# The second layer of a gated feed-forward stage with its weights stationary and its output turned back

## The chip, the cores and the metric

The kernel runs on one core of one Trainium2 chip. The metric is the time of one execution on the device, in microseconds (us). Busy times and orders of events come from a trace of one profiled execution.

## The reference

A small network works on x of shape 16 x 16 x 16 x 64: 4096 tokens of 64 channels, 16 images of 256 tokens. It has eight steps in a row, each preceded by a normalization and added to its input. The change touches the second, `L0_ffn`. It runs on 8 "rows" in its own set-up, but on 16 images here (s = 256 tokens, D = 64, H = 256):

```python
weights = (jnp.einsum('bsd,do->bso', x, wr) + br)[..., 0]
k = max(1, int(CAPACITY * s))
kk = k - 1 if k > 1 else 1
_, idx = jax.lax.top_k(weights, k)
sel_idx = idx[:, :kk]
sel = jnp.take_along_axis(x, sel_idx[:, :, None], axis=1)
h = jax.nn.gelu(jnp.einsum('bkd,dh->bkh', sel, w1) + b1)
y = jnp.einsum('bkh,hd->bkd', h, w2) + b2
w_sel = jnp.take_along_axis(weights, sel_idx, axis=1)
y = y * w_sel[..., None]
...
return processed + x
```

For each image the 127 tokens with the largest router weight go through a layer of 256 with a gelu and a layer back to 64, with the bias b2, and are scaled with the router weight. All is float32.

## The kernel before

All 4096 tokens stay in SBUF for the whole kernel, in X. They are worked on in 8 blocks of 512 tokens (BLK; four tiles t of 128 tokens, two images). The eight steps are eight stages s = 0 to 7, one after the other, each with its own body for every engine; a stage runs over the blocks two at a time: `trips` makes a hardware loop of three trips and a fourth trip written out, with u = 0 for even blocks and u = 1 for odd ones. Engines are ordered only by semaphores, and each executes its own instructions in the order written.

Besides the stage's own work each block carries two other things:

- The preparation of a block ahead (of b + 2, or of the next stage's first). VectorE takes the statistics of X (`prep_stats`), GpSimd makes rstd by a power (`prep`, L643), VectorE writes V (`prep_norm`, L1651), TensorE transposes V (`turn_v`, L1065), ScalarE copies it to VS (L701), and VectorE writes the rounding rest into VS's other half (`prep_split`, L1672), which raises vt_ready.
- A step of a power iteration on small matrices that a later stage needs, cut into pieces. TensorE has slot1 and slot2 in even blocks and slot3 in odd ones, each behind it a small copy by ScalarE (T, U, msum) and a segment on GpSimd: seg1 (ends with bsq, L500, which slot2 needs), seg2 (which slot3 needs) and seg3. GpSimd's order in an even block is seg1, rstd, seg2; in an odd block seg3, rstd.

The stage that is changed is `topk_stage` (s = 1). TensorE computes for a block the router row (rep_hi and rep_lo, into bank 2 + u), then the first layer with W1 stationary and 512 tokens moving (two halves c of the 256 hidden units, into banks 0 and 1), waits for vt_ready of the next block, issues slot1 or slot3, and then the second layer: `hid` holds gelu's output as [128 hidden, 512 tokens] for each c (L776, ScalarE), and for each tile t its 128 x 128 piece is the stationary operand and W2b the moving one, with b2 added by a matmul of one row of ones (L1139, L1140). So the output y comes with tokens on partitions, in bank 4 + u. VectorE meanwhile finds for each token by comparisons whether it is among the kept (L1735 to L1752), makes coef from it, XV = X + V, writes V of the block ahead, waits for l2_done, and computes X = XV + y * coef (L1757, L1759), which raises block_done. l2_done also tells ScalarE when `hid` may be overwritten.

`fold` is a [128, 64] matrix of two identities, one above the other (L1581): stationary data of [128, 128 tokens] with fold moving gives, for 128 tokens, the sum of the upper and the lower 64 rows, turned. Stages 3, 5 and 7 end with it (L1397). `ct` is a tile of the seventh stage.

Of the kernel before, what the change touches and what calls it, by code (L numbers as in the profile page):

```python
# [21 lines left out]
ACT = mybir.ActivationFunctionType  # L22
AX = mybir.AxisListType

P = 128
C = 64
IMG = 16
NT = 4
# [3 lines left out]
NB = 8  # L32
# [16 lines left out]
CREDIT = 2  # L49
# [22 lines left out]
def metaformer(nc, a, out):  # L72
    ctx = ExitStack()
    with ctx:
        def sb(name, shape, dt=F32):
            return ctx.enter_context(nc.sbuf_tensor(name, shape, dt))

        def sem(name):
            return ctx.enter_context(nc.semaphore(name))

        banks = ctx.enter_context(nc.psum_tensor("banks", [P, 8, 512], F32))
        bank = [banks[:, i, :] for i in range(8)]
# [32 lines left out]
        ones = sb("ones", [P, PIX])  # L115
# [32 lines left out]

        W2b = sb("W2b", [P, 2, C])
        b1b = sb("b1b", [P, 2])  # L150
        b2b = sb("b2b", [1, C])
        wrow = sb("wrow", [P, BLK])
        wcol = sb("wcol", [P, NT])
        above = sb("above", [P, NT])
# [3 lines left out]
        tmp = sb("tmp", [P, NT, C])  # L158
# [34 lines left out]
        hid = view(scratch, 0, (4, BLK))  # L193
# [17 lines left out]
        fold = sb("fold", [P, C])  # L211
# [16 lines left out]
        ct = sb("ct", [P, BLK])  # L228
# [51 lines left out]
        block_done = sem("block_done")  # L280
# [7 lines left out]
        h_ready = sem("h_ready")  # L288
        l2_done = sem("l2_done")
        y_ready = sem("y_ready")  # L290
        logits_ready = sem("logits_ready")
        lg_ready = sem("lg_ready")
        ex_ready = sem("ex_ready")
# [41 lines left out]
        def row(ap):  # L335
            return ap.rearrange("(o n) -> o n", o=1)

        def col(ap):
            return ap.rearrange("(n o) -> n o", o=1)

        def bcast(ap, n):
# [9 lines left out]
        ]  # L351
        loads = [
            (W2b[:], a["L0_ffn_w2"].rearrange("(n p) c -> p n c", p=P)),
            (b1b[:], a["L0_ffn_b1"].rearrange("(n p) -> p n", p=P)), (b2b[:], row(a["L0_ffn_b2"])),
            (omb[0:3 * TAPS, :], col(a["L1_conv_om_bias"])),
            (bg[3][:], bcast(a["L1_ffn_gate_b"], P)),
            (W2[3][:], a["L1_ffn_W2"].rearrange("e h c -> h e c")),
# [79 lines left out]
        def _(pool):  # L437
# [7 lines left out]

            pool.memset(OMK_cols[:].bitcast(F32), 0.0)
            pool.memset(omb[:], 0.0)
            pool.memset(W2[5][:], 0.0).then_inc(w2_zeroed, 1)
            pool.memset(ones[:], 1.0)
            pool.memset(neghalf[:], -0.5)  # L450
# [246 lines left out]
        def _(act):  # L697
# [79 lines left out]

            def topk_stage(i, s, s_next, wrap):
                for u in range(2):
                    for c in range(2):  # L780
                        hidden(i, u, s, c, ACT.Gelu_apprx_tanh, b1b[:, c:c + 1])
                    (slot1 if u == 0 else slot3)(i + STEP0[s])
                    if u == 0:
                        slot2(i + STEP0[s])
                    prep_ahead(i, u, s, s_next, wrap)
# [207 lines left out]
        def _(pe):  # L993
            pe.sem_inc(v_turned, CREDIT)
            pe.sem_inc(l2_done, 4)
            pe.sem_inc(s_used, 3)


# [2 lines left out]
            for k in range(TAPS):  # L1001
                ins = pe.transpose(bank[k // 8][0:C, (k % 8) * C:(k % 8 + 1) * C], Ko[:, :, k], ident[0:C, 0:C])
# [121 lines left out]
            def topk_stage(i, s, s_next, wrap):  # L1124
                for u in range(2):
                    b = i * 2 + u
                    pe.wait_ge(vt_ready, b + (NB * s + 1))
                    pe.wait_ge(block_done, b + (NB * s + 1))
                    exact(bank[2 + u][:, :], rep_hi[:, 2, :], rep_lo[:, 2, :], u).then_inc(b_row, 1)
                    for c in range(2):  # L1130
                        pe.wait_ge(h_ready, i * 4 + (2 * u + c + 1))
                        exact(bank[c][:, :], W1_hi[1][:, c, :], W1_lo[1][:, c, :], u).then_inc(h_psum, 1)
                    pe.wait_ge(vt_ready, b + (NB * s + 2))
                    (slot1 if u == 0 else slot3)(i + STEP0[s])
                    pe.wait_ge(h_ready, i * 4 + (2 * u + 2 + CREDIT))
                    for t in range(NT):
                        y = bank[4 + u][:, t * C:(t + 1) * C]
                        for c in range(2):
                            pe.matmul(y, hid[:, 2 * u + c, t * P:(t + 1) * P], W2b[:, c, :], start=(c == 0), stop=False)  # L1139
                        ins = pe.matmul(y, ones[0:1, 0:P], b2b[:], start=False, stop=True)  # L1140
                    ins.then_inc(l2_done, 2)
                    if u == 0:
                        slot2(i + STEP0[s])
                    pe.wait_ge(ch_act, i * 3 + (3 * STEP0[s] + 4 + u))
                    prep_ahead(prep, i, u, s, s_next, wrap)
# [399 lines left out]
        def _(vec):  # L1545
            steps = [0]

            def mark(ins):

                steps[0] += 1  # L1550
                ins.then_inc(vec_step, 1)
# [5 lines left out]
            def link(ins):  # L1557

                mark(ins)
                settle()  # L1560
# [170 lines left out]
            def topk_stage(i, s, s_next, wrap):  # L1731
                for u in range(2):
                    b = i * 2 + u
# [12 lines left out]
                    for t in range(NT):  # L1746
# [5 lines left out]
                    mark(vec.scalar_tensor_tensor(coef[:], above[:], float(KEEP), wcol[:], ALU.is_lt, ALU.mult))  # L1752
                    link(vec.tensor_tensor(XV[:], xblock(b), V[u][:], ALU.add))
                    ahead(prep_norm, i, u, s, s_next, wrap)
                    vec.wait_ge(l2_done, i * 4 + (2 * u + 2 + 4))
                    settle()
                    link(vec.tensor_tensor(tmp[:], bank[4 + u][:, 0:NT * C].rearrange("p (t c) -> p t c", t=NT),  # L1757
                                           coef[:].rearrange("p (t o) -> p t o", o=1).to_broadcast([P, NT, C]), ALU.mult))
                    vec.tensor_tensor(xblock(b), XV[:], tmp[:], ALU.add).then_inc(block_done, 1)  # L1759
                    ahead(prep_split, i, u, s, s_next, wrap)  # L1760
# [290 lines left out]
```

## Time and profile before

| | |
|---|---|
| median of 3 runs | 1260.85 us (1257.79 to 1271.09) |
| the profiled execution | 1254.95 us, span 1253.2 us |
| mean granted TensorE clock | 0.841 |
| TensorE busy | 993.4 us (79%) |
| VectorE busy | 705.2 us (56%) |
| ScalarE busy | 478.2 us (38%) |
| GpSimd busy | 458.7 us (37%) |
| group L1139, TensorE, 128 records | 32.7 us in the stage |
| group L1140, TensorE, 64 records | 20.5 us in the stage |

A float32 matmul leaves two records on TensorE. Weight loads (PEld) overlap the matmuls. "Idle before <- X" says how long the engine had been idle and what released it. Line numbers are those of this kernel.

### The profile page before, as it was taken

The numbers are of one execution on the slowest core, as the hardware profiler recorded it, in microseconds if no ns is written. First come the engines' busy times: TensorE is split into PE (matmuls) and PEld (weight loads), VectorE is DVE, ScalarE is ACT, GpSimd is POOL, SyncE is SP. The second block draws the span as 40 slices with busy tenths as digits, with TensorE's granted clock in tenths as the row PEclk, the third lists the DMA queues.
The fourth block names the chain that finished last, engine by engine and source line by source line (L and its number), as shares of the span: only waits on it lengthen the run. The fifth ranks groups of instructions, "written<-read, shape, count | busy, mean of one in ns | idle before, by whom it ended". The sixth has DMA issues, their size and how long they took to land.

```text
span 1253.2 us, 17519 instructions
## 1 busy us (share of the span) xinstructions
PE 993.4 (79%) x4690; PEld 607.0 (48%) x4690; DVE 705.2 (56%) x2469; ACT 478.2 (38%) x903; POOL 458.7 (37%) x1308
## 2 busy tenths in 40 slices
PE   2444368877789899888888987779899566899998
PEld 2444356665455455554444444545555444444443
DVE  3555756554455555544366565667665543666653
ACT  1222201113544555544254444433434111466665
POOL 4555535654054333454542431125554310111010
PEclk9999999555799987988976787787877766899999
DMA  4400000000000000000000000000000000000000
GB/s 72 78 0 0 1 1 0 0 1 1 1 1 1 0 0 0 0 0 2 1 1 0 0 0 1 0 1 1 0 0 1 0 0 1 1 9 4 8 4 9
DMA packets 26340, 6.27 MB, mean 5 GB/s; under 512 B 24054, under 2 KB 26230, under 8 KB 26294
## 3 DMA queue, kind: packets, MB, share of 16 engines
q1 hardware_dynamic: 26294, 5.73, 2.5%
q8 instruction: 20, 0.33, 0.1%
q14 instruction: 26, 0.21, 0.1%
HBM read 4.68 MB, written 1.05 MB: 5 GB/s over the span
## 4 chain that ended last, share of the span: by engine, by line
PE 44%; issue 13%; DVE 10%; ACT 4%; POOL 2%; DVEq 0%; ACTq 0%; POOLq 0%
PE banks L1373 7%; PE banks L1200 6%; PE banks L1091 4%; PE banks L1092 3%; PE banks L1022 3%; PE banks L1500 3%; PE banks L1390 2%; PE banks L1397 2%; PE banks L1192 2%; DVE V L1651 2%; PE banks L1341 2%; DVE weighted L1913 2%; DVE summed L1917 2%; PE banks L1155 1%; PE banks L1176 1%
## 5 line engine op out<-in xcount | busy, mean ns | idle before, releaser
L903 ACT ACTIVATE scratch<-banks,b 128x512 f32<-128x512 f32 x224 | 144.6, 683 | 57.1 <-PE banks L1092 53.9
L1373 PE MATMUL banks<-scratch,W 128*64 128x512 f32 (+1 forms) x448 | 157.3, 688 | 0.5
L1808 DVE TENSOR_TENSOR scratch<-banks,XR 128x1024 f32<-128x1024 f32 x72 | 87.5, 1224 | 103.5 <-PE banks L1192 76.5
L1091 PE MATMUL banks<-VS,W_hi 128*128 128x512 f32 x240 | 121.8, 507 | 2.2 <-DVE X L1982 1.0
L643 POOL TENSOR_TENSOR rstd<-vareps,neghalf 128x4 f32<-128x4 f32 x64 | 67.5, 1054 | 136.8 <-DVE vareps L1639 131.2
L701 ACT ACTIVATE VS<-banks 64x256 fp32r<-64x256 f32 x112 | 42.5, 379 | 190.2 <-PE banks L1065 175.0
L1065 PE MATMUL banks<-ident,V 128*128 128x128 f32 x128 | 33.1, 348 | 93.8 <-DVE V L1651 90.7
L1092 PE MATMUL banks<-VS,W_lo 128*128 128x512 f32 x240 | 107.3, 447 | 0.0
L1913 DVE SCALAR_TENSOR_TENSOR weighted<-banks,b,cwide 128x512 f32<-128x512 f32 x72 | 53.9, 749 | 86.4 <-PE banks L1373 85.8
L1651 DVE TENSOR_SCALAR V<-X,moments,rstd 128x64 f32 (+1 forms) x256 | 62.9, 309 | 57.1 <-POOL rstd L643 35.5
L1200 PE MATMUL banks<-scratch,region 128*64 128x256 f32 x576 | 90.3, 440 | 3.6 <-DVE scratch L1808 3.6
L914 ACT ACTIVATE cwide<-banks 128x512 f32<-128x512 f32 x96 | 57.4, 598 | 86.7 <-PE banks L1390 86.4
L1091 PEld LDWEIGHTS banks<-VS,W_hi 128*128 128x128 f32 x240 | 51.6, 215 | 53.8 <-issue 28.6
L1672 DVE TENSOR_TENSOR VS<-banks,VS 64x256 fp32r<-64x256 f32 x112 | 47.4, 423 | 52.4 <-ACT VS L701 50.8
L1065 PEld LDWEIGHTS banks<-ident,V 128*128 128x128 f32 x128 | 15.4, 164 | 119.5 <-DVE V L1651 82.4
L652 POOL TENSOR_TENSOR ex<-euler,lg 128x32 f32<-128x32 f32 x8 | 43.5, 5432 | 80.2 <-DVEq L1875 80.0
L558 POOL TENSOR_TENSOR cp<-U,qv 64x18 f32<-64x18 f32 x40 | 8.8, 239 | 147.4 <-ACT U L739 147.4
L655 POOL TENSOR_TENSOR ex<-euler,m 128x4 f32<-128x4 f32 x16 | 16.3, 1020 | 119.8 <-DVEq L1883 119.8
L1200 PEld LDWEIGHTS banks<-scratch,region 128*64 128x64 f32 x576 | 38.8, 151 | 40.6 <-issue 25.1
L1092 PEld LDWEIGHTS banks<-VS,W_lo 128*128 128x128 f32 x240 | 53.0, 221 | 6.4
L1390 PE MATMUL banks<-cwT,select 16*128 16x512 f32 x96 | 54.0, 563 | 1.1 <-ACT cwT L908 1.1
L1373 PEld LDWEIGHTS banks<-scratch,W 128*64 128x64 f32 (+1 forms) x448 | 33.6, 156 | 40.1 <-issue 25.9
(280 smaller groups left out, 2114.9 us busy)
## 6 DMA issues: line engine op xcount, KB each, us to landing
X<-in_x SPq DMA_DIRECT2D x8, 128.0 KB, 2.6
region<-in_L_ffn_W SPq DMA_DIRECT2D x2, 512.0 KB
out<-X SPq DMA_DIRECT2D x8, 128.0 KB, 2.0
W<-in_L_ffn_W SPq DMA_DIRECT2D x1, 512.0 KB
region<-in_L_ffn_W SPq DMA_DIRECT2D x2, 256.0 KB
scratch<-in_L_conv_kernel SPq DMA_DIRECT2D x2, 144.0 KB
W<-in_L_ffn_W SPq DMA_DIRECT2D x1, 256.0 KB
region<-in_L_ffn_w SPq DMA_DIRECT2D x2, 128.0 KB
```

The lines of the kernel that those rows point to most:

```text
L643: pool.tensor_tensor(rstd[:], vareps[:], neghalf[:], ALU.pow).then_inc(rstd_ready, 1)
L903: act.activation(hid[:, c % 4, :], bank[c % 2][:, :], ACT.Gelu, bias=b1[s][:, w:w + 1]).then_inc(h_ready, 1)
L914: act.activation(cwide[:, j, :], bank[4][:, :], ACT.Copy).then_inc(wide_copied, 1)
L1065: ins = pe.transpose(bank[6][:, m * P:(m + 1) * P], V[u][:, 2 * m:2 * m + 2, :].rearrange("p t c -> p (t c)"), ident[:])
L1091: pe.matmul(out, hi, VS[u][:], start=True, stop=False)
L1092: return pe.matmul(out, lo, VS[u][:], start=False, stop=True)
L1200: ins = pe.matmul(bank[1][m * C:(m + 1) * C, 0:PIX], Z[v][:, 2 * m + h, k * C:(k + 1) * C], S[:, k % 3, h, m * PIX:(m + 1) * PIX], start=( ...
L1373: ins = pe.matmul(y, W2[s][:, w, :], hid[:, c % 4, :], start=opens, stop=closes, skip_group_check=True)
L1390: pe.matmul(bank[4][:, :], select[:, j, :], cwT[:], start=True, stop=True).then_inc(wide_psum, 1)
L1651: ins = vec.tensor_scalar(V[u][:, place, :], X[:, bass.ds(b * NT + t, 1), :].rearrange("p o c -> p (o c)"), moments[:, t, 0:1], rstd[:, t: ...
L1808: vec.tensor_tensor(S[:, k % 3], pair(p), xr, ALU.mult).then_inc(s_ready, 1)
L1913: vec.scalar_tensor_tensor(weighted[:] if j else summed[u][:], bank[2 + j % 2][:, :], b2[s][:, j:j + 1], cwide[:, j, :], ALU.add, ALU.mult ...
```

## The change

W2b becomes the stationary operand: for each half c of the hidden units one matmul with 64 columns takes `hid` of 512 tokens as the moving operand, and writes into 64 of the 128 partitions of bank 5 (c = 0 the lower, c = 1 the upper). ScalarE copies the bank to `ct` and adds b2 on the way; b2b is now a column of 128 with zeros in its second half, so that it is added once. Four matmuls with `fold` sum the two halves and turn them back, into bank 4 for every block. Two new semaphores, pair_copied and pair_turned, carry the hand-over.

```diff
-        b2b = sb("b2b", [1, C])
+        b2b = sb("b2b", [P, 1])
...
+        pair_copied = sem("pair_copied")
+        pair_turned = sem("pair_turned")
...
-            (b1b[:], a["L0_ffn_b1"].rearrange("(n p) -> p n", p=P)), (b2b[:], row(a["L0_ffn_b2"])),
+            (b1b[:], a["L0_ffn_b1"].rearrange("(n p) -> p n", p=P)), (b2b[0:C], col(a["L0_ffn_b2"])),
...
+            pool.memset(b2b[:], 0.0)
...
             def topk_stage(i, s, s_next, wrap):
                 for u in range(2):
+                    b = i * 2 + u
                     for c in range(2):
                         hidden(i, u, s, c, ACT.Gelu_apprx_tanh, b1b[:, c:c + 1])
                     (slot1 if u == 0 else slot3)(i + STEP0[s])
+                    act.wait_ge(l2_done, i * 4 + (2 * u + 2 + 4))
+                    act.wait_ge(pair_turned, b + 1)
+                    act.activation(ct[:], bank[5][:, :], ACT.Identity, bias=b2b[:]).then_inc(pair_copied, 1)
                     if u == 0:
                         slot2(i + STEP0[s])
...
+            pe.sem_inc(pair_turned, 1)
...
                     pe.wait_ge(h_ready, i * 4 + (2 * u + 2 + CREDIT))
+                    for c in range(2):
+                        pe.matmul(bank[5][c * C:(c + 1) * C, :], W2b[:, c, :], hid[:, 2 * u + c, :],
+                                  start=True, stop=True, skip_group_check=True).then_inc(l2_done, 1)
+                    pe.wait_ge(pair_copied, b + 1)
+                    pe.wait_ge(block_done, b + (NB * s + CREDIT))
                     for t in range(NT):
-                        y = bank[4 + u][:, t * C:(t + 1) * C]
-                        for c in range(2):
-                            pe.matmul(y, hid[:, 2 * u + c, t * P:(t + 1) * P], W2b[:, c, :], start=(c == 0), stop=False)
-                        ins = pe.matmul(y, ones[0:1, 0:P], b2b[:], start=False, stop=True)
-                    ins.then_inc(l2_done, 2)
+                        ins = pe.matmul(bank[4][:, t * C:(t + 1) * C], ct[:, t * P:(t + 1) * P], fold[:],
+                                        start=True, stop=True)
+                    ins.then_inc(pair_turned, 1)
...
-                    vec.wait_ge(l2_done, i * 4 + (2 * u + 2 + 4))
+                    vec.wait_ge(pair_turned, b + 2)
                     settle()
-                    link(vec.tensor_tensor(tmp[:], bank[4 + u][:, 0:NT * C].rearrange("p (t c) -> p t c", t=NT),
+                    link(vec.tensor_tensor(tmp[:], bank[4][:, 0:NT * C].rearrange("p (t c) -> p t c", t=NT),
```

On TensorE, in an even block of the stage's loop, slot1's matmuls, the second layer and slot2 stand like this before (a row is one instruction, or several alike; `scratch` is hid, and REGISTER_ALU computes the value of a wait):

```order
L1022 MATMUL banks<-va,Ko 64x2 x9
L1135 REGISTER_ALU
L1139 MATMUL banks<-W2b,scratch 128x64 [waits h_ready]
L1139 MATMUL banks<-W2b,scratch 128x64
L1140 MATMUL banks<-b2b,ones 128x64
L1139 MATMUL banks<-W2b,scratch 128x64 x2
L1140 MATMUL banks<-b2b,ones 128x64
```

And in the changed kernel, whose lines are numbered 7 to 10 higher here:

```order
L1030 MATMUL banks<-va,Ko 64x2 x9
L1143 REGISTER_ALU
L1145 MATMUL banks<-scratch,W2b 64x512 [waits h_ready]
L1145 MATMUL banks<-scratch,W2b 64x512
L1147 REGISTER_ALU
L1150 MATMUL banks<-fold,ct 128x64 [waits block_done,pair_copied]
L1150 MATMUL banks<-fold,ct 128x64 x3
```

Of 12 matmuls 6 are left, between the same neighbours, with one wait among them.

On ScalarE, in the same even block, from the second gelu to the copy of V's transposes, before:

```order
L776 ACTIVATE scratch<-banks,b1b 128x512 [waits l2_done,h_psum]
L730 ISA
L731 ACTIVATE T<-banks 64x18 [waits ch_pe]
L736 REGISTER_ALU
L738 ACTIVATE U<-banks 64x9 [waits ch_pe]
L739 ACTIVATE U<-banks 64x18
L712 ISA
L701 ACTIVATE VS<-banks 64x2x128 [waits v_turned]
```

And in the changed kernel:

```order
L779 ACTIVATE scratch<-banks,b1b 128x512 [waits l2_done,h_psum]
L733 ISA
L734 ACTIVATE T<-banks 64x18 [waits ch_pe]
L787 REGISTER_ALU
L788 ISA [waits l2_done]
L789 ACTIVATE ct<-banks,b2b 128x512 [waits pair_turned]
L739 REGISTER_ALU
L741 ACTIVATE U<-banks 64x9 [waits ch_pe]
L742 ACTIVATE U<-banks 64x18
```

One copy of a whole bank is put between T (slot1's result) and U (slot2's), with no table load beside it.

## Rows read from the trace of the kernel before

**Rows 1.** Busy time in five blocks: stretch, length, each engine's busy us (instructions), PEclk, DMA
```profile
175.69:191.24 15.55, 15.15 (x72) 13.00 (x72) 9.48 (x45) 2.56 (x7) 3.94 (x11) 1.00 0.00 1
...
207.30:222.30 15.00, 14.59 (x73) 12.30 (x73) 10.19 (x47) 2.56 (x7) 6.42 (x23) 0.72 0.00 0
222.30:238.77 16.47, 11.28 (x39) 9.19 (x39) 8.68 (x44) 2.33 (x5) 12.33 (x38) 0.50 0.00 0
238.77:254.57 15.80, 15.39 (x72) 13.03 (x73) 10.19 (x47) 2.56 (x7) 6.53 (x24) 0.50 0.00 0
...
286.08:296.73 10.65, 9.15 (x38) 7.26 (x39) 7.55 (x33) 4.03 (x7) 7.66 (x25) 0.66 0.00 1
```

**Rows 2.** Timeline, TensorE, block 4 (start us, us, engine, line, tiles, count)
```profile
244.93 1.12 PE L1139 MATMUL banks<-W2b,scratch 128*128 128x64 f32 x4
...
251.57 0.58 PE L1042 MATMUL banks<-bsq,ones 64*128 64x2 f32 x2
```

**Rows 3.** Timeline, the other engines in block 4
```profile
248.34 0.19 POOL L500 TENSOR_TENSOR bsq<-vb 64x2 f32<-64x2 f32 x1
...
249.83 0.98 DVE L1651 TENSOR_SCALAR V<-X,moments,rstd 128x64 f32 x4 [1.62 <-POOL rstd L643]
251.68 0.42 DVE L1757 TENSOR_TENSOR tmp<-banks,coef 128x256 f32<-128x256 f32 x1 [0.87 <-PE banks L1140]
...
254.28 0.17 ACT L739 ACTIVATE U<-banks 64x18 f32<-64x18 f32 x1
```

**Rows 4.** Waits in block 3 (who waited for whom: us, times, longest)
```profile
DVE V L1651 <- POOL rstd L643: 6.0, 1, 6.0
...
PE banks L1065 <- DVE V L1651: 5.2, 1, 5.2
```

**Rows 5.** Timeline, block 2
```profile
216.86 0.19 POOL L500 TENSOR_TENSOR bsq<-vb 64x2 f32<-64x2 f32 x1
...
219.30 0.58 PE L1042 MATMUL banks<-bsq,ones 64*128 64x2 f32 x2
```

**Rows 6.** Timeline, TensorE, a later stage, granted clock 0.50
```profile
664.99 1.80 PE L1397 MATMUL banks<-fold,summed 128*128 128x64 f32 x8
666.73 0.79 PE L1390 MATMUL banks<-cwT,select 16*128 16x512 f32 x1
...
670.96 1.98 PE L1373 MATMUL banks<-scratch,W 128*64 128x512 f32 x4
672.87 0.79 PE L1390 MATMUL banks<-cwT,select 16*128 16x512 f32 x1
```

**Rows 7.** Timeline, TensorE: two groups at the full clock, one full-width matmul at half
```profile
642.54 1.08 PE L1373 MATMUL banks<-scratch,W 128*64 128x512 f32 x4
...
648.09 1.10 PE L1397 MATMUL banks<-fold,summed 128*128 128x64 f32 x8
...
908.93 2.05 PE L1373 MATMUL banks<-scratch,W 128*128 128x512 f32 x2
```

**Rows 8.** Timeline, the third stage: hand-overs from TensorE to ScalarE and back
```profile
300.84 0.68 ACT L790 ACTIVATE omt<-banks,omb 64x512 f32<-64x512 f32 x1 [9.03 <-PE banks L1155]
...
301.69 1.91 PE L1161 MATMUL banks<-fold_quads,omt 64*128 64x32 f32 x8
...
320.59 3.74 PE L1155 MATMUL banks<-VP,OMK_cols 128*64 128x512 f32 x9
...
324.37 0.68 ACT L790 ACTIVATE omt<-banks,omb 64x512 f32<-64x512 f32 x1 [2.63 <-PE banks L1155]
```

**Rows 9.** Timeline, the end of block 7 and the next stage's start
```profile
295.75 0.42 DVE L1757 TENSOR_TENSOR tmp<-banks,coef 128x256 f32<-128x256 f32 x1 [1.29 <-PE banks L1140]
...
304.02 1.33 POOL L643 TENSOR_TENSOR rstd<-vareps,neghalf 128x4 f32<-128x4 f32 x1 [0.17 <-POOL qv L494]
...
306.23 0.88 DVE L1651 TENSOR_SCALAR V<-X,moments,rstd 128x64 f32<-128x64 f32 x4
```

**Rows 10.** Timeline, ScalarE, block 7
```profile
290.53 1.28 ACT L978 ACT_TABLE_LOAD   x1
```

## What was predicted, before the changed kernel had run

> **What bounds the kernel now.** The change touches one of eight stages, the token gate's feed-forward part (`topk_stage`, "the stage" below), which runs from 175.7 to 296.6 us: eight blocks, an even one (u=0) and an odd one (u=1) in turn. I read first the busy time by block [rows 1]. A block takes 15.0 to 16.5 us whatever its kind. In even blocks TensorE is busy almost throughout (15.39 of 15.80 us), in odd ones it is not (11.28 of 16.47), while GpSimd is busy 12.33 us of the odd block and 6.53 of the even one. So two different chains set the two kinds of block, and the change can be worth something only where TensorE's does.
>
> Then the order of time in block 4, an even one [rows 2, 3]. TensorE's second layer, the group that the change replaces, runs from 244.93 until the next instruction starts at 251.57: 6.64 us for 12 matmuls, which leave 24 records. Right behind it come slot2 (251.57 on), ScalarE's copy of U (ends 254.45) and the transposes of the block after next (254.57, the end of this window in [rows 1]). Nothing in between waits for another engine: GpSimd had bsq, which slot2 needs, at 248.53, and VectorE had V, which the transposes need, at 250.81. VectorE waited 0.87 us for the group. The even block is TensorE's chain, and the group is on it.
>
> In block 3, an odd one, the waits [rows 4] tell another story: V waited 6.0 us for GpSimd's rstd, and the transposes waited 5.2 us for V. GpSimd was in seg3, which starts when slot3's result is copied; slot3 is issued ahead of the second layer. The group could be 5 us shorter or longer there and nothing would move.
>
> The clock: the granted clock of [rows 1] is 0.50 (1.2 GHz) in blocks 3 and 4 and partly higher in 2 and 7. Block 0 is listed at 1.00, but is as long as block 4 (15.55 against 15.80), so I take the slow durations for it too. In block 2 the fast stretch was worth some 0.5 to 0.8 us (15.00 against 15.55 and 15.80).
>
> **The change, part by part.** Prices are those of the slow clock, from rows of later stages that do the same thing.
>
> 1. Removed: 12 matmuls on the array, 6.64 us per block [rows 2].
> 2. Added: two matmuls with W2 stationary, 64 columns each, 512 activations moving, into the two column halves. An expert pair (L1373) is exactly this. In the slow clock its four records take 1.98 us [rows 6]. One matmul of the full 128 columns took 2.05 us for two records [rows 7], so the halves cost together what one full matmul costs; I take 1.98.
> 3. Added: the wait for ScalarE and back. The nearest case is omt (L790), Identity with a bias from PSUM. TensorE's last matmul ended at 324.33 and ScalarE started at 324.37; it took 0.68 us for 512 columns; in the slow clock TensorE's next load started 0.17 us after such a copy ended [rows 8]. Together 0.04 + 0.68 + 0.17 = 0.89 us.
> 4. Added: four fold products. L1397 has that shape: 1.80 us, 1.74 until the next instruction starts [rows 6]. Its first load was ahead of time there, and with the wait it won't be; the four turns behind omt took 1.91 [rows 8]. I take 1.85.
> 5. Sum: 1.98 + 0.89 + 1.85 = 4.72 us against 6.64, so 1.92 us less per block.
>
> ScalarE is cheap to use: it is busy 2.56 us of an even block [rows 1]. Behind the new copy on its queue stand U's copy in even blocks, whose matmuls are later on TensorE anyway, and the next VS copy in odd ones, which waits for the transposes. Behind the copy of block 7 stands a table load, needed only in the next stage [rows 10]. No other table load is added.
>
> The single bank 4 makes the fold products wait for block_done of the block before. That came before vt_ready of the next block, on which TensorE already waits ahead of slot1 or slot3, because VectorE splits after it adds. So this costs nothing; if VectorE came late it would be seen first at vt_ready. VectorE's own wait moves from l2_done to pair_turned, same place. The memset of one more column and a load of 64 small pieces in place of one row are hidden: they belong to the loads at the kernel's start, and the stage starts at 175.7 us.
>
> *Even blocks.* After the cut slot2 would start at 251.57 - 1.92 = 249.65 in block 4. bsq is there at 248.53. The transposes would come at 252.65, V is there at 250.81. VectorE's tmp would start right behind V, at about 250.9, still ahead of the next block. So the whole 1.92 us comes through, and what is late next is slot2 behind bsq, 1.1 us further down. Block 2 is the tightest: its group began in a fast stretch, slot2 at 219.30 and bsq done at 217.05 [rows 5], with room for about 2.1 us. Four even blocks: 4 x 1.92 = 7.7 us.
>
> *Odd blocks.* Blocks 1, 3 and 5: 0.
>
> *Block 7* has no block to prepare in this stage; its output starts the next one. VectorE waited 1.29 us for the group there [rows 9], so 1.29 is the most that can be won before VectorE's own work is the end. A part of it meets GpSimd: in the next stage rstd ended at 305.35 and V started 0.88 us later, so no more than 0.9 passes. Its group ran partly fast, where the cut is smaller. I take 0.5.
>
> **Sum:** 7.7 + 0.5 = 8.2 us off the profiled execution's 1254.95 us, so 1246.7. The median of the runs is 5.9 us above that execution; off the median it is 1252.6 us, 0.65% less.
>
> *Bounds of the unknown prices.* High price: give the way to ScalarE and back 1.7 us and the group is 5.5, worth 1.1 per even block, 4.4 in all. Low price: at the full clock the pair takes 1.08 and the fold products 1.10 [rows 7]; a group of 3.0 would save 3.6, but slot2 then stands behind bsq (room of 3.0 us in block 4, 2.2 in block 2), so at most 2.2 to 3.0 per even block, about 11, and 12 with block 7.
>
> A rule that would price item 2 otherwise: TensorEngine Tiling in the Trainium skill says under Key Properties that changing the tiling mode drains TensorE, and this change makes it switch to half-width tiles and back in every block. The rows of the expert pair contain both switches already (a full-width matmul before and after), so the sum stays at 1.98; if the drain were extra, it would eat into the 1.92.
>
> **The rivals.**
>
> *A, the forecast:* even blocks gain, odd ones don't. 8 us, between 4 and 11. Chance 0.68.
>
> *B, the clock comes up as well.* The pair streams 512 columns where the old matmuls streamed 64, behind the first layer's six 512-column streams. The fast stretches of blocks 2 and 7 [rows 1] followed such streams. If each of the four even blocks got one, that is 4 x 0.7 = 2.8 more, 11; if it held through slot1, the group and slot2, the odd blocks' start up to slot3 would shorten too, 13 to 20 off: 1241 to 1248. For: the denser stream. Against: a new gap of 0.9 us, then 64-column products and slot2 again. TensorE: Matmul & The Clock Gate in the Trainium skill (Part 1) has it that activity releases the throttle, and that small idle times between groups can make it swing; so it speaks for both. Chance 0.14.
>
> *C, nothing to be seen:* a gain under 4 us, because the group is nearer 5.7, or the fast stretches of blocks 2 and 7 are lost (about 1.5 us), or the room before bsq is eaten. 1257 to 1261. Chance 0.13.
>
> *D, slower.* The hand-over through ScalarE costs more than the group saved: this decides from 0.89 + 1.92 = 2.8 us between the pair's end and the first fold product. If ScalarE had to change tables for Identity and back for Gelu (1.28 us each [rows 10]), in each even block 2.6 us would be added to TensorE's chain, 4 x (2.6 - 1.9) = 3 us slower, about 1264. Against: Copy runs between Gelus in this stage, and Identity beside Exp and Copy in the next, without loads, and the program has none. Chance 0.05.
>
> **The numbers.** I call 1% (12.6 us) what can be told from no change here. A and C stay within it; of B somewhat more than half passes it, and A's tail with a lucky median a little, so faster 0.13; D passes it only if the loads also stall the odd blocks, slower 0.03; the rest, 0.84, within. The range: up to 1260 it holds A, most of C; down to 1243 it holds most of B.
>
> **What would show it.** Right: in even blocks the group takes about 4.7 us, of which 0.9 between pair and fold products; even blocks of about 13.5 to 14 us, odd ones still 16; V's wait for rstd in odd blocks as before, TensorE's wait for V there near 7 us in place of 5. Block 7's tmp no longer waits. Stages after it as long as before. Wrong: slot2 waiting for GpSimd in even blocks (my room was too small); a granted clock above 0.6 over most of the stage (B); fold products starting over 1.5 us after the pair (C or D); odd blocks that change their length by more than 0.5 us at the same clock.

## The result and the profile after

The changed kernel takes 1250.43 us (median of 20 runs, 1243.67 to 1260.70), the kernel before 1264.59 us in 20 runs beside them. The ratio is 0.9929, with a 95% interval of 0.9899 to 0.9958: 0.7% faster, 9 us. It is less than the 14.2 us between the two medians, because all ratios here compare fast runs alone, those within 1.5% of the fastest of their kernel, and six of the 20 runs before are slower than that. The forecast was 8.2 us less (0.65%) and 1252.6 us.

The profiled execution of the changed kernel has a span of 1245.2 us against 1253.2. Here is the busy time by block, as in [rows 1]: blocks 0, 2, 3, 4 and 7, the columns being the stretch, its length, and the busy time (instructions) of TensorE, its weight loads, VectorE, ScalarE and GpSimd, then the granted clock and DMA.

```profile
175.72:188.54 12.82, 11.53 (x60) 9.08 (x61) 9.39 (x45) 3.24 (x8) 4.22 (x11) 0.75 0.00 1
...
204.52:218.47 13.95, 12.65 (x60) 9.42 (x61) 10.10 (x47) 3.25 (x8) 6.20 (x23) 0.50 0.00 0
218.47:235.02 16.55, 8.52 (x27) 5.57 (x27) 8.76 (x44) 3.02 (x6) 12.33 (x39) 0.50 0.00 0
235.02:248.95 13.93, 12.63 (x60) 9.40 (x61) 10.10 (x47) 3.24 (x8) 6.20 (x23) 0.50 0.00 0
...
278.98:289.38 10.40, 8.51 (x26) 5.59 (x27) 7.54 (x33) 4.83 (x8) 7.11 (x23) 0.50 0.00 1
```

Block 4, wholly at the slow clock in both kernels, went from 15.80 to 13.93 us. Block 3, an odd one, went from 16.47 to 16.55, though TensorE has 2.8 us less to do in it. The stage takes 113.7 us in place of 121.0.

Block 4 in TensorE's order of time, where [rows 2] stood before, and ScalarE's copy:

```profile
241.18 1.97 PE L1145 MATMUL banks<-scratch,W2b 128*64 128x512 f32 x4
244.05 1.97 PE L1150 MATMUL banks<-fold,ct 128*128 128x64 f32 x8 [0.89 <-ACT ct L789]
245.95 0.58 PE L1050 MATMUL banks<-bsq,ones 64*128 64x2 f32 x2
```

```profile
243.31 0.69 ACT L789 ACTIVATE ct<-banks,b2b 128x512 f32<-128x512 f32 x1 [1.84 <-PE banks L1145]
```

The group takes 4.77 us from its first matmul to slot2 (245.95 - 241.18): 1.97 for the pair, 0.89 idle for the hand-over (TensorE gives the bank to ScalarE and gets ct back), the rest the fold products.

The limits that come next in block 4, where [rows 3] stood, on GpSimd and VectorE:

```profile
244.59 0.19 POOL L503 TENSOR_TENSOR bsq<-vb 64x2 f32<-64x2 f32 x1
```

```profile
246.08 0.99 DVE L1662 TENSOR_SCALAR V<-X,moments,rstd 128x64 f32 x4 [1.62 <-POOL rstd L646]
246.97 0.42 DVE L1768 TENSOR_TENSOR tmp<-banks,coef 128x256 f32<-128x256 f32 x1
```

bsq is there at 244.78, 1.2 us before slot2 takes it; VectorE no longer waits for the output. And the waits of block 3, where [rows 4] stood:

```profile
PE banks L1073 <- DVE V L1662: 7.1, 1, 7.1
DVE V L1662 <- POOL rstd L646: 6.0, 1, 6.0
```

V still waits 6.0 us for rstd, and what TensorE saved it now spends on waiting for V (7.1 us, before 5.2).

### The profile page after: what moved, and what is told of

Its sections match the earlier page's. It is cut to its first block, busy times and chain, and to the rows that moved or that the text cites. A ratio compares the mean times of both kernels' runs of the same rounds, so it can differ in the third digit from the quotient of the medians.

```text
span 1245.2 us, 17359 instructions
## 1 busy us (share of the span) xinstructions
PE 968.5 (78%) x4594; PEld 581.0 (47%) x4594; DVE 704.5 (57%) x2469; ACT 484.4 (39%) x911; POOL 459.9 (37%) x1309
## 3 DMA queue, kind: packets, MB, share of 16 engines
HBM read 4.68 MB, written 1.05 MB: 5 GB/s over the span
## 4 chain that ended last, share of the span: by engine, by line
PE 45%; issue 12%; DVE 9%; ACT 4%; POOL 4%; DVEq 0%; ACTq 0%; POOLq 0%
PE banks L1384 7%; PE banks L1211 6%; PE banks L1099 4%; PE banks L1030 3%; PE banks L1100 3%; PE banks L1511 2%; PE banks L1401 2%; PE banks L1203 2%; DVE V L1662 2%; PE banks L1408 2%; PE banks L1352 2%; PE banks L1166 1%; PE banks L1199 1%; PE banks L1187 1%; PE banks L1195 1%
## 5 line engine op out<-in xcount | busy, mean ns | idle before, releaser
L1384 PE MATMUL banks<-scratch,W 128*64 128x512 f32 (+1 forms) x448 | 154.2, 666 | 0.4
L1073 PE MATMUL banks<-ident,V 128*128 128x128 f32 x128 | 33.4, 352 | 102.6 <-DVE V L1662 99.5
L1073 PEld LDWEIGHTS banks<-ident,V 128*128 128x128 f32 x128 | 15.7, 165 | 129.7 <-DVE V L1662 90.8
```

The lines of the kernel that those rows point to most:

```text
L1073: ins = pe.transpose(bank[6][:, m * P:(m + 1) * P], V[u][:, 2 * m:2 * m + 2, :].rearrange("p t c -> p (t c)"), ident[:])
L1384: ins = pe.matmul(y, W2[s][:, w, :], hid[:, c % 4, :], start=opens, stop=closes, skip_group_check=True)
```

## Experiments

Below, a stage's length runs from block 1's transposes (the last that the stage before issues) to the next stage's first matmul, and a block's from the transposes that its predecessor issues to those that it issues itself; block 7 ends with the next stage's first matmul. The table is worked out from the starts of L1073 (L1065 before) in each kernel's trace.

```
kernel                              stage   block 0     1     2     3     4     5     6     7
before                              121.0     15.56 16.05 15.00 16.47 15.80 15.99 15.52 10.65
changed                             113.7     12.82 15.98 13.95 16.55 13.93 16.47 13.56 10.40
e1 new group in even blocks         115.5     13.69 16.53 13.02 15.92 13.97 16.47 13.56 12.35
e2 new group in odd blocks          120.3     15.56 15.61 15.81 16.55 15.79 15.93 15.51  9.50
e3 bias on VectorE, old operands    109.5     12.83 16.29 12.84 15.97 12.86 15.98 12.77  9.95
e4 changed, rstd ahead of seg3      104.9     12.80 10.65 16.91 10.66 16.97 10.66 16.72  9.50
e5 changed, no hand-over            109.3     12.81 15.96 12.99 16.51 12.97 15.61 12.81  9.66
e6 changed, odd pair three times    113.5     12.81 16.50 13.95 16.50 13.94 16.02 13.55 10.19
e7 changed, even pair twice         117.2     14.34 15.60 15.71 16.51 13.77 15.61 15.26 10.40
e8 changed, rstd ahead, two stages  106.6     13.70 10.66 16.95 10.66 16.94 10.66 16.59 10.40
e9 before, one bias matmul          114.3     12.81 16.50 13.94 16.51 13.93 16.51 13.62 10.47
e10 before, bias with 128 rows      116.2     12.93 16.50 14.65 16.50 14.48 15.92 14.18 11.03
e11 before, rstd ahead, two stages  109.0     14.65 11.21 16.95 11.21 16.71 11.22 16.74 10.31
e12 e3, rstd ahead, two stages      105.4     12.81 10.65 16.99 10.66 16.96 10.66 16.72  9.95
```

Lengths of one kind of block differ by 0.5 to 1.1 us where a stretch ran at the full clock. Each row is one profiled execution. e5, e6, e7 and e10 ran only that once, so for them there are blocks and stages but no ratio.

### Even blocks or odd ones

e1 has the new group under `if u == 0:` and the old one under `else:`, e2 the reverse. The new group stands where the diff has "...". In both, b2 is loaded in both forms, and the semaphores count only the blocks that use them:

```diff
+                    if u == 0:
...
+                    else:
+                        for t in range(NT):
+                            y = bank[4 + u][:, t * C:(t + 1) * C]
+                            for c in range(2):
+                                pe.matmul(y, hid[:, 2 * u + c, t * P:(t + 1) * P], W2b[:, c, :], start=(c == 0), stop=False)
+                            ins = pe.matmul(y, ones[0:1, 0:P], b2row[:], start=False, stop=True)
+                        ins.then_inc(l2_done, 2)
```

> The new group only in even blocks, the old one in odd blocks (and so in block 7). Stage lengths are from block 1's transposes to the next stage's first matmul: 121.0 us in the kernel before, 113.7 in the changed one. If the gain comes from TensorE's chain in the even blocks alone, all of it is here: the stage takes about 114 us (even blocks 13.9, odd ones 16 to 16.5), and the whole 8 us less than before. If every shortened group counts alike, there is half of it: about 117.4 us and 4 us less.

> The reverse: the new group only in odd blocks. If odd blocks wait for GpSimd's seg3, nothing is gained: the stage takes 120.5 to 121.5 us (block 7 may give 0.3 of it), the time is that of the kernel before. If every shortened group counts alike: about 117.4 us and 4 us less.

e1: 0.9923 of the kernel before (0.9885 to 0.9961), the same as the whole change. e2: 1.0006 (0.9972 to 1.0039), nothing. The blocks say it more sharply: block 4 takes 13.97 us in e1 and 15.79 in e2; block 3 takes 15.92 in e1, with the old group, and 16.55 in e2, with the new one, where e1 had a fast stretch in it (granted clock 0.61 against 0.50). So the gain is TensorE's chain in even blocks. The stage of e2 is 120.3 us, 0.2 below what was expected; its block 7, with the new group, took 9.50 us against 10.65.

The stage of e1 was to be about 114 us and is 115.5. The 1.9 us over the changed kernel's stage are block 7: 12.35 us with the old group, 10.40 with the new one; the differences of the other blocks cancel. VectorE's wait for the old group in e1's block 7:

```profile
290.22 0.42 DVE L1781 TENSOR_TENSOR tmp<-banks,coef 128x256 f32<-128x256 f32 x1 [3.00 <-PE banks L1161]
```

It is 3.00 us where the profiled execution before had 1.29 [rows 9], because part of that group had run at the full clock. At the slow clock the change is worth 1.95 us in block 7, up to the next stage's first matmul. Little of that is left further on. The next stage's first transposes, which wait for V, came 21.60 us after block 7's start in e1 (300.45 - 278.85) and 21.06 in the changed kernel (300.04 - 278.98): 0.54 us, and e1 ran partly at the full clock in between.

```profile
300.45 0.41 PE L1075 MATMUL banks<-ident,V 128*128 128x128 f32 x2 [2.44 <-DVE V L1672]
```

```profile
300.04 0.66 PE L1073 MATMUL banks<-ident,V 128*128 128x128 f32 x2 [3.24 <-DVE V L1662]
```

In the changed kernel V waits there for GpSimd's rstd:

```profile
298.91 0.99 DVE L1662 TENSOR_SCALAR V<-X,moments,rstd 128x64 f32<-128x64 f32 x4 [0.56 <-POOL rstd L646]
```

### More work in the groups

e6 adds two more pairs of W2 matmuls ahead of the pair in odd blocks, whose result the pair overwrites; e7 adds one pair, in even blocks (2 * 1 if u == 0).

```diff
+                    for c in range(2 * 2 if u == 1 else 0):
+                        pe.matmul(bank[5][c % 2 * C:(c % 2 + 1) * C, :], W2b[:, c % 2, :], hid[:, 2 * u + c % 2, :],
+                                  start=True, stop=True, skip_group_check=True)
```

> The changed kernel, and in odd blocks the pair of matmuls is issued three times (3.8 us more on TensorE in each odd block; the same result). TensorE waited 7.1 us for V there, so blocks 1, 3 and 5 keep their 16 to 16.5 us and the wait falls to about 3.3. Block 7, also odd, prepares nothing and has no such room: it takes the 3.8 us, 14.2 in place of 10.4. The stage: about 117.5. If odd groups counted like even ones, it would be 113.7 + 4 x 3.8 = 129.

> The changed kernel, and in even blocks the pair of matmuls is issued twice (1.9 us more in each). If TensorE's chain sets the even blocks all of it shows: 15.8 us in place of 13.9, the stage 121.3, as long as in the kernel before. If there is room in the even blocks too, less.

e6: with two pairs more, blocks 1, 3 and 5 keep their 16.0 to 16.5 us. The two pairs took 3.5 us in block 3, but the last pair and the fold products ran at the full clock (1.11 and 1.10 us in place of 1.98 and 1.97), so TensorE had only 1.8 us more to do there, and its wait for V fell to 5.4 us, not to 3.3. Block 7 didn't behave as expected: it stayed at 10.19 us, and the stage at 113.5 in place of 117.5. Its three pairs ran at the full clock (eight records in 1.94 us, and TensorE's fold products in 1.11), so the extra work cost little there.

```profile
283.14 1.94 PE L1145 MATMUL banks<-scratch,W2b 128*64 128x512 f32 x8 [0.52 <-ACT scratch L779]
284.91 1.03 PE L1148 MATMUL banks<-scratch,W2b 128*64 128x512 f32 x4
286.75 1.11 PE L1153 MATMUL banks<-fold,ct 128*128 128x64 f32 x8 [0.81 <-ACT ct L789]
```

e7: 1.76 us more in block 2 (13.95 to 15.71), 1.70 in block 6 and 1.52 in block 0, nearly the 1.9 expected. But block 4 took 13.77 us, less than without the extra pair. After the second pair its fold products and slot2 ran at the full clock (slot2's 18 records in 1.27 us, against 2.08 in the slow clock):

```profile
245.66 1.88 PE L1148 MATMUL banks<-scratch,W2b 128*64 128x512 f32 x4
248.44 1.10 PE L1153 MATMUL banks<-fold,ct 128*128 128x64 f32 x8 [0.90 <-ACT ct L789]
249.48 0.38 PE L1050 MATMUL banks<-bsq,ones 64*128 64x2 f32 x2
249.79 1.27 PE L1030 MATMUL banks<-vb,Ki 64*64 64x2 f32 x18
```

This speaks for rival B's mechanism, that a longer wide stream can bring the clock up. In e6 all four odd blocks had a fast stretch from the third pair or earlier, where the changed kernel had one in block 1 alone. But that is not shown: each kernel was profiled once, fast stretches also came in block 5 of e2, e5 and e10, which have no extra pair, and the granted clock over the stage is 0.62 in e6 but 0.57 in e7, against 0.56 in the changed kernel. In e7 the extra pair paid for itself in one block of four, and the stage took 117.2 us against 113.7. In the changed kernel the granted clock was 0.50 in blocks 2 to 7, and the stage owes nothing to it but in blocks 0 and 1.

### What the group is made of

e5 takes the hand-over out: the fold products read a constant tile, ScalarE's copy runs beside them.

```diff
-                    pe.wait_ge(pair_copied, b + 1)
...
-                        ins = pe.matmul(bank[4][:, t * C:(t + 1) * C], ct[:, t * P:(t + 1) * P], fold[:],
+                        ins = pe.matmul(bank[4][:, t * C:(t + 1) * C], before[:].rearrange("p t n -> p (t n)")[:, t * P:(t + 1) * P], fold[:],
...
+                    pe.wait_ge(pair_copied, b + 1)
                     pe.wait_ge(ch_act, i * 3 + (3 * STEP0[s] + 4 + u))
```

> The changed kernel, but the fold products read a tile of constants in place of ct, so they need not wait for ScalarE (the copy still runs); this leaves the second layer's output out. The group shrinks by the hand-over of 0.89 us, from 4.77 to about 3.9. In even blocks slot2 then meets its next limit, GpSimd's bsq: with the bias on VectorE the even blocks were 12.84 us and slot2 waited for GpSimd. So the even blocks should go from 13.9 to 12.9 to 13.1 us, the odd ones stay at 16 to 16.5, the stage comes to 109.5 to 110.5. If the hand-over was hidden anyway, nothing moves (113.7).

Block 4 took 12.97 us against 13.93, 0.96 less for a hand-over of 0.89; the stage 109.3. In block 4 bsq was there only 0.2 us before slot2 (243.48 and 243.70). The hand-over is on the path in full. That is the price of letting ScalarE stand between the two products.

e3 keeps the old operands and only drops the four bias matmuls per block:

```diff
-                                pe.matmul(y, hid[:, 2 * u + c, t * P:(t + 1) * P], W2b[:, c, :], start=(c == 0), stop=False)
-                        ins = pe.matmul(y, ones[0:1, 0:P], b2b[:], start=False, stop=True)
+                                ins = pe.matmul(y, hid[:, 2 * u + c, t * P:(t + 1) * P], W2b[:, c, :], start=(c == 0), stop=(c == 1))
...
                     link(vec.tensor_tensor(tmp[:], bank[4 + u][:, 0:NT * C].rearrange("p (t c) -> p t c", t=NT),
+                                           b2b[:].rearrange("p (o c) -> p o c", o=1).to_broadcast([P, NT, C]), ALU.add))
+                    link(vec.tensor_tensor(tmp[:], tmp[:],
```

> The kernel before with the hidden activations still stationary; only the four bias matmuls per block are gone, VectorE adds b2 with one instruction more (0.43 us) before it multiplies. Eight of twelve matmuls are left, 16 of 24 records, 4.43 us at the slow clock against 4.77 measured for the new group. If only the length of TensorE's group in even blocks matters, this gains as much as the change or slightly more: even blocks 13.6 us, the stage 112.5 to 113.5 us, the whole 8 to 9 us less than before. If the turned operands themselves bring the gain (wide moving streams, a better clock), it is below 4 us.

e3: 0.9905 (0.9869 to 0.9941), and the stage is 109.5 us, 4 us shorter than in the changed kernel and below what was expected. Whole times don't tell the two apart (0.9929 for the change). The eight matmuls alone took 3.67 us, not the 4.43 of their share. In block 6, where they ran faster still, slot2 met the limit named in the prediction: it waited 1.23 us for GpSimd.

```profile
239.75 3.67 PE L1139 MATMUL banks<-W2b,scratch 128*128 128x64 f32 x16
243.44 0.59 PE L1042 MATMUL banks<-bsq,ones 64*128 64x2 f32 x2
```

```profile
272.29 0.56 PE L1042 MATMUL banks<-bsq,ones 64*128 64x2 f32 x2 [1.23 <-POOLq L553]
```

So of the old group's 6.64 us the four bias matmuls, with one row of ones each, were 2.97, or 0.74 apiece, more than the 0.46 of a W2 matmul with 128 rows. The change's gain in the group is all theirs: turning the operands replaced 3.67 us by 4.77, and only because the bias went to ScalarE does the new group come out 1.87 us shorter. Two more kernels ask why they are dear. e10 leaves them in place and gives them all 128 rows (ones[:, 0:P] and a tile that is zero below its first row). e9 uses one of 256 columns that opens the bank (b2b then holds b2 four times):

```diff
+                    pe.matmul(bank[4 + u][:, 0:NT * C], ones[0:1, 0:P], b2b[:], start=True, stop=False, skip_group_check=True)
                     for t in range(NT):
                         y = bank[4 + u][:, t * C:(t + 1) * C]
                         for c in range(2):
-                            pe.matmul(y, hid[:, 2 * u + c, t * P:(t + 1) * P], W2b[:, c, :], start=(c == 0), stop=False)
-                        ins = pe.matmul(y, ones[0:1, 0:P], b2b[:], start=False, stop=True)
+                            ins = pe.matmul(y, hid[:, 2 * u + c, t * P:(t + 1) * P], W2b[:, c, :], start=False,
+                                            stop=(c == 1), skip_group_check=True)
```

> The kernel before, where the four bias matmuls stay in their places but take all 128 rows: ones as the stationary operand, and a tile with b2 in its first row and zeros below as the moving one. The same count of matmuls, columns and records. If the one-row shape between full ones is what costs, each of the four now costs what a W2 matmul costs, 0.46 us: a group of 5.4 to 5.6 us in place of 6.64, even blocks about 14.7. If it is only their number, 6.64 and 15.8 stay.

> The kernel before, where one bias matmul of one row and 256 columns opens the whole bank and the eight W2 matmuls add to it, in place of four bias matmuls of 64 columns between them. The eight alone took 3.67 us at the slow clock, with the four between them 6.64, so each of the four cost 0.74 us, more than the 0.46 of a W2 matmul. If what costs is going to one row and back, which now happens once in a block: a group of 4.4 to 4.6 us, even blocks about 13.7 us, as good as the changed kernel without a copy on ScalarE. If the columns cost, the one matmul costs as much as the four together and nothing is won (6.6).

e10's group, from block 4, two of its four tiles and the next instruction:

```profile
242.27 1.11 PE L1140 MATMUL banks<-W2b,scratch 128*128 128x64 f32 x4
243.18 0.64 PE L1141 MATMUL banks<-b2b,ones 128*128 128x64 f32 x2
...
247.02 0.64 PE L1141 MATMUL banks<-b2b,ones 128*128 128x64 f32 x2
247.58 0.58 PE L1043 MATMUL banks<-bsq,ones 64*128 64x2 f32 x2
```

It takes 5.31 us (247.58 - 242.27), 1.33 less than with one row, for the same number of matmuls, columns and records (5.4 to 5.6 was expected; even blocks behind the first took 14.2 to 14.7 us). The weight loads show a difference. With one row, in the kernel before, the bias matmul's load and the next W2 load begin no earlier than their matmuls do (245.98 and 246.59); in e10 the bias matmul's load begins 0.10 us ahead of its matmul (243.08 and 243.18):

```profile
245.98 0.50 PEld L1140 LDWEIGHTS banks<-b2b,ones 1*128 1x128 f32 x2
246.59 0.93 PEld L1139 LDWEIGHTS banks<-W2b,scratch 128*128 128x128 f32 x4
```

```profile
243.08 0.55 PEld L1141 LDWEIGHTS banks<-b2b,ones 128*128 128x128 f32 x2
```

e9's group:

```profile
241.49 1.22 PE L1136 MATMUL banks<-b2b,ones 1*128 1x256 f32 x2
242.63 3.67 PE L1140 MATMUL banks<-W2b,scratch 128*128 128x64 f32 x16
246.24 0.58 PE L1042 MATMUL banks<-bsq,ones 64*128 64x2 f32 x2
```

4.75 us (246.24 - 241.49), a little over the 4.4 to 4.6 expected, and 0.9924 of the kernel before (0.9892 to 0.9957): as good as the change, with neither a turned output nor a copy on ScalarE. The one-row shape between full ones costs 0.33 us each time in the slow clock (1.33 / 4). TensorEngine Tiling in the Trainium skill (Key Properties) says that changing the tiling mode drains TensorE. If a one-row matmul is such a change, e10 and the loads agree with that, but no run here tells a drain from another reason why the load isn't taken ahead. Nor does one isolate it for the half-width tiles of the new pair, whose 1.97 us includes it.

### Odd blocks, and a faster kernel

e4 moves one call on GpSimd in this stage; e8 does so in the first stage too (`()` in place of `(0,)`). seg3 then comes behind the step that makes rstd.

```diff
             def body(i, s, s_next, wrap):
...
-                    if s in (0, 1) and second_half:
+                    if s in (0,) and second_half:
                         seg3(step)
...
-                    if s not in (0, 1) and second_half:
+                    if s not in (0,) and second_half:
                         seg3(step)
```

> The changed kernel, and in this stage GpSimd computes rstd for the block ahead before seg3 in place of behind it. If odd blocks are set by seg3 ahead of rstd, V and the transposes come some 5 us earlier there, until slot1 of the next block waits for seg3's end: 3 to 3.6 us less in each of blocks 1, 3 and 5, the stage about 103 to 105 us and the whole 9 to 11 us less than the changed kernel (some 18 less than before). If something else holds the odd blocks, or seg3's later start by 1.4 us costs as much as the earlier V gives, nothing: the stage stays at 113 to 115 us.

> The changed kernel with rstd ahead of seg3 on GpSimd in this stage and in the first one, whose odd blocks have the same order. In this stage as with the change in this stage alone (104.9 us, odd blocks 10.7, even ones 16.9). If the first stage's odd blocks also wait for rstd behind seg3, it gets some us shorter and the whole falls below 1240; if not, the time is that of the kernel with the move in one stage, 0.986 of before.

e4: 0.9864 of the kernel before (0.981 to 0.9918), the stage 104.9 us. The odd blocks fall from 16.5 to 10.66 us, the even ones rise to 16.9, since seg3's end is now waited for by slot1 and bsq comes later:

```profile
204.35 0.38 PE L1044 MATMUL banks<-ones 64*128 64x1 f32 x2 [1.75 <-POOLq L618]
...
213.03 0.58 PE L1050 MATMUL banks<-bsq,ones 64*128 64x2 f32 x2 [1.28 <-POOLq L556]
```

A pair of blocks takes 27.6 us against 30.5. That shows what held the odd blocks. The even blocks' 3 us were not in the expectation as such, but its sum was right (3 us less for each pair). e8: 0.9738 (0.9687 to 0.979), median 1229.09 us, the fastest kernel of this study. In the first stage the odd blocks' transposes had waited 11.19 us for V and now wait 5.61. In e8, the transposes of an even block and then those of the odd one behind it:

```profile
42.72 0.69 PE L1073 MATMUL banks<-ident,V 128*128 128x128 f32 x2 [0.41 <-ACT U L742]
55.73 0.69 PE L1073 MATMUL banks<-ident,V 128*128 128x128 f32 x2 [5.61 <-DVE V L1662]
```

In the changed kernel these two started at 42.75 and 61.34, so 5.6 us came off each of three such blocks. The changed stage took 106.6 us in e8, not the 104.9 of e4, because blocks 0 and 7 had no fast stretch of that size.

e11 and e12 ask what the second layer's group is worth once GpSimd's order is mended: e11 is the kernel before with the same move, e12 is e3 with it.

> The kernel before, with its old second layer, and rstd ahead of seg3 in both stages. With the new group and this move, slot2 waited 1.3 us for GpSimd's bsq in even blocks: bsq came 5.9 us after slot1's end, because GpSimd was late. The old group takes 6.64 us, only some 0.7 us longer than that. So the change is worth at most 0.7 us in each of the four even blocks here and about 2 in block 7, 3 to 5 us in all in place of 8 to 9: 0.977 of before, against 0.974 with the new group. If the change keeps its worth whatever GpSimd does, it is 0.981.

> Rstd ahead of seg3 in both stages, and the kernel before's second layer without its bias matmuls, b2 added on VectorE. Its group takes 3.67 us against 4.77 of the new one, but in even blocks both end before bsq, so they should be alike: even blocks 16.9 us, odd ones 10.7, the time within 1 us of the kernel with the new group (0.974 of before). If the group still mattered there, 4 us less.

In the stage, e11 takes 109.0 us, e8 106.6, e12 105.4. The old group costs 0.55 us in each of three odd blocks (11.2 against 10.66) and little or nothing in blocks 2, 4 and 6, where slot2 waits for GpSimd with the new one. So within the stage the change is worth 2.4 us here, in place of 7.4. That is less, as expected, but below the 3 to 5 us of the expectation and made up otherwise: it had 0 for odd blocks (measured 1.7 in all) and about 2 for block 7 (measured -0.1, where e11 had a fast stretch). e12's blocks 1 to 6 are those of e8 to 0.1 us or so, as expected.

The whole times say something else: e11 is at 0.9809 (0.9784 to 0.9833), which is the 0.981 that the expectation gave to the rival, that the change keeps its worth. e12 is at 0.9757 (0.9733 to 0.9781), e8 at 0.9738, and e8's interval and e11's just overlap. e11 and e12 ran beside each other, e8 at another time on another chip. Between e11's and e8's profiled executions 12 us differ, of which only 2.4 lie before the third stage; the other 10 are in stages with the same instructions. Those stages, first in e8, then in e11:

```profile
265.61:1223.40 957.79, 815.04 (x3886) 458.57 (x3886) 532.98 (x1705) 426.10 (x742) 304.99 (x799) 0.83 0.01 2
```

```profile
268.00:1235.50 967.50, 828.91 (x3886) 462.74 (x3886) 533.51 (x1705) 425.32 (x742) 304.46 (x798) 0.82 0.01 2
```

The same 3886 records kept TensorE busy 14 us longer in e11, at a lower granted clock (0.82 against 0.83), while VectorE, ScalarE and GpSimd took what they took in e8. So the 10 us go with TensorE's clock, and are not work that the old group adds. In e12 those stages took 964.2 us. Two of e8's runs had the granted clock of e11's (0.82) and took 1234.1 and 1234.2 us, 3 to 4 us less than e11's median of 1237.7, which is nearer to the stage's 2.4. Why the clock was granted less in all of e11's runs (1236 to 1243 us) stays open, and so does what the change is worth in the whole time with this order on GpSimd.

## Why the prediction was right

**What bounds the stage.** Right on both kinds of block. Even blocks are TensorE's chain (e1, e5, e7's block 2), odd ones GpSimd's seg3 ahead of rstd (e2, e6, e4).

**The group.** Expected 4.72 us, measured 4.77: pair 1.98 and 1.97, hand-over 0.89 and 0.89, fold products 1.85 and 1.90. The pair came from a row of the same shape and clock. The 1.85 was a choice between 1.74 (same shape, first load ahead of time) and 1.91 (another shape). The hand-over's sum was right by luck, its parts were not. Expected were 0.04 us from the pair's end to ScalarE, 0.68 for the copy and 0.17 back; measured in block 4 are 0.16 (243.15 to 243.31), 0.69 and 0.05 (244.00 to 244.05). The 0.17 was not the way back alone: when that load started [rows 8], TensorE was still in L1176's matmuls (301.32 to 301.76).

**What passes through.** Expected 1.92 in each even block, 7.7 in four. Measured 2.74, 1.05, 1.87 and 1.96, together 7.6. Only blocks 4 and 6 compare like with like; block 0 gained from a fast stretch in the changed kernel, block 2 lost the one it had had. That they cancel is luck.

**Odd blocks.** Expected 0; measured 0.07, -0.08 and -0.48, together -0.5. The last is a fast stretch that the kernel before had in block 5 (granted clock 0.61) and the changed one hadn't.

**Block 7.** I took 0.5 us: of a wait of 1.29, no more than 0.9 was to pass GpSimd. The 1.29 was too short, from an execution in which the old group had run partly at the full clock; at equal clock 1.95 us are won up to the next stage's first matmul (e1). But 0.54 of them is left at the next stage's first transposes, where V waits for GpSimd's rstd as the forecast had it. So 0.5 fits there, though e1's full clock in between has a part in that. In this pair of executions the two figures are 0.25 and 0.12, since the fast stretch was gone. The sum over the stage, 7.6 - 0.5 + 0.25 = 7.4 us, is 0.8 below the 8.2 of the forecast. The full span differs by 8.0; the other 0.7 is in later stages with the same instructions, and stands for nothing.

**The whole time.** 1250.43 us against 1252.6. The kernel before was 3.7 us slower in these 20 runs (1264.59) than in the three that the forecast started from (1260.85), so the ratio is the fairer test: 0.7% against 0.65%.

**The room before bsq.** Expected 1.1 us in block 4, found 1.2. e5 and e3 use it up but for 0.2 and 0.1 us in block 4, and in e3's block 6 slot2 waits; their even blocks take 12.8 to 13.0 us.

**Rival B** (the clock comes up) didn't happen in the changed kernel; e6 and e7 speak for it with more pairs and don't prove it. **C** is out as a time, but one of its conditions came true: the fast stretches of blocks 2 and 7 were lost in the profiled execution. **D** is out: the hand-over was 0.89 us in six blocks and 0.81 in blocks 6 and 7, and ScalarE loaded no table for it.

What I had not weighed was where the old group's 6.64 us came from. I treated its 24 records as alike, and so made e3's expectation 0.76 us too long. The busy times of L1139 and L1140 before already told them apart: 32.7 us for 128 records and 20.5 for 64, so 0.51 and 0.64 us for one matmul.

## What to carry to other kernels

Look up which chain sets each kind of block before pricing an edit: here the same 1.9 us on TensorE was worth everything in four blocks and nothing in three, and one moved call on GpSimd, in two stages, was worth 24 us without the change (e11) where the change was worth 9. A one-row bias matmul between full ones is dear, 0.74 us against 0.46 for a full one here; add the bias once for the bank (e9), or on the engine that reads it (e3). Take prices from rows at the same clock, the waits too: a wait in a profiled execution that had a fast stretch is too short for the others.

## What the runs showed of the hardware

- Two matmuls of 64 columns in two column halves, 512 moving, take 1.97 us at 1.2 GHz, about as long as one of 128 columns (2.05 [rows 7]).
- A float32 matmul with 128 rows, 128 columns stationary and 64 moving costs 0.46 us in a row of such (e3). One with one row of ones between them costs 0.74 us (before against e3), and with 128 rows in the same place 0.33 us less (e10).
- For ScalarE's copy of a bank (0.69 us) between two of its groups TensorE stood idle 0.81 to 0.89 us in every block of the changed kernel.
- With one more wide pair, TensorE came to 2.4 GHz behind it in one of e7's four even blocks, and that block was shorter (13.77 us) than without it (13.93). Whether the pair was the cause is not shown.
- Between executions, stages with the same instructions differ: from the third stage's start to the end it was 956.5 us before, 955.8 in the changed kernel and 967.5 in e11, with TensorE busy 819.5, 814.2 and 828.9 us for the same 3886 records. A few us in one stage are seen in the trace, not in a single whole time.
